# A two-layer graph network on one core: edges counted by 16 destinations in pairs of windows, other banks for the first source rows, branch arms exchanged

## The chip, the cores and the metric

One core of one Trainium2 chip. The metric is the device time of one execution in microseconds (us), median of the runs. The kernel is written for the five engines directly: each engine has a program of its own and they meet at semaphores only. TensorE is called PE in the rows (PEld is its weight load), VectorE DVE, ScalarE ACT, GpSimd POOL, SyncE SP.

## The reference

1,250 nodes with 768 features, 40,000 edges (src, dst) sorted by dst, and a self loop for each node. Two blocks, each followed by a residual and a layer norm:

```
x_norm = layer_norm(x)
out1 = gat_conv(x_norm, ...)        # 4 heads of 192; softmax over the edges of a dst
out2 = gat_conv(out1, ...)          # 2 heads of 96
x = layernorm(x + (concat([x, out2]) @ Wu + bu))
h = relu(gcn_conv(x, W1, b1))       # out[dst] += (x @ W)[src] * dinv[src] * dinv[dst]
x = layernorm(x + gcn_conv(h, W2, b2))
```

Every sum over edges depends on the graph only through how often a pair (src, dst) occurs. So the kernel first makes the dense matrix of counts, 1280 x 1280, and turns both layers into dense products with it.

## The kernel before

**Counting.** The edges lie in 313 chunks of 128; two chunks are a *unit* (157 units). The destinations are cut into 40 *windows* of W = 32, four for each of T = 10 tiles of 128. Since the edges are sorted, a window needs a short run of units. For each unit VectorE compares (`one_hots`): `src_hot`, for each edge which of 128 low source numbers it has (256 elements, two chunks), and `dst_hot`, for each edge which of 320 pairs (source tile, destination in the window) it has (640 elements). TensorE multiplies the two per chunk (`mm`, 320 columns, bf16) and adds all units of a window in one PSUM bank (`edge_window`). UW = 4 units are written out in a ring of RING = 4 slots (names `ohs_*`, `ohd_*`); what a window needs beyond them runs in a loop with run-time bounds (`xohs`, `xohd`), at least once a window. The bounds come from a small table in SBUF (`rngrow`), made at the start by VectorE from the smallest and largest destination of each chunk, and read into registers (`TENSOR_LOAD rngrow`) by TensorE and VectorE. A matmul with the identity adds the self loops. ScalarE copies the bank into `ctmp`.

**What lies between.** After each window of a tile TensorE does a quarter of the first layer's dense product (`wp`, `xT`, three matmuls, six records), after the first one also the ten transposes of the previous tile's counts (`count_transposes`); ahead of a tile it transposes the normalised rows (`normal_transposes`), and ScalarE copies them to `xT` in six pieces. The last tile does its product in two windows, twelve records each.

**Handover.** When the source scores of all tiles are there, VectorE splits them in two parts (`svec`), TensorE transposes them and broadcasts them over the partitions (`source_rows`, ten matmuls for one head into three banks), ScalarE copies the three pieces (`source_piece`), and VectorE takes 10 maxima a head (`maximum`), 40 in all, then starts the attention. Beside this TensorE does `x_transposes` and `x_wu` (the product of x with Wu).

**GCN.** A register says whether any degree is over 4096. If so, `messages` and `gcn` run in plain f32, otherwise with every number in a high and a low part. Here it is the second. In `first_layer` six column blocks f of 128 are summed over ten source tiles q: `pair(q)` does blocks 0 and 1 beside the preparation of tile q, `sums(2, q)` the third block, which uses the other banks (0, 1, 5); block 3 needs the banks of blocks 0 and 1 (2, 3, 4) back.

An engine's program is a fixed order; no scheduler is involved.

## Time and profile before

| | |
|---|---|
| three runs | 804.77, 807.14, 807.78 us; median 807.14 |
| profiled execution | 806.62 us, of it span 804.9 |
| busy in the span | PE 768.4 us, DVE 579.0, ACT 321.1, POOL 23.3 |
| counting (about 41 to 202 us) | PE full, DVE 75 to 95% |
| maxima and first attention (204 to 305) | DVE full |
| other attention, GCN (305 to 800) | PE full but for short gaps |

A busy PE is a model: its records overlap, and what a matmul costs is the distance of its start to the next start. "Idle before, releaser" at a row's end says how long the engine stood still ahead of that instruction and what ended it.

### The profile page before, as it was taken

To read this page: it belongs to the slowest core of one execution; us is meant where nothing else is said; L and a number is where in the kernel's file an instruction comes from. 1 tells how busy PE (TensorE), PEld (TensorE's weight loads), DVE (VectorE), ACT (ScalarE), POOL (GpSimd) and SP (SyncE) were. 2 spreads that over 40 slices of the span, in tenths; PEclk is the share of its full clock that TensorE was granted. 3 is DMA by queue.
4 is the path that set the end of the run, shared out by engine and by line. 5 is a ranking of instruction groups with operands and counts; after the bars stand their busy time and mean duration, and the time that the engine had idled before them with its cause. 6 is when DMAs were issued, how large, how long until landed. Compare 5 with 4: busy or idle time off the path is not lost.

```text
span 804.9 us, 11740 instructions
## 1 busy us (share of the span) xinstructions
PE 768.4 (95%) x4215; PEld 651.9 (81%) x4215; DVE 579.0 (72%) x1143; ACT 321.1 (40%) x638; POOL 23.3 (3%) x38
## 2 busy tenths in 40 slices
PE   5999999999999989999999999899999999999997
PEld 4966666665665989999966788799799999999996
DVE  2699988886899999999689999795553432403554
ACT  4537666754533334343253555562203331301000
POOL 6100000000000010000000020000000000000000
PEclk9999999999989999999989999999999999999999
DMA  9400000000000132020000510100000003000121
GB/s 314 159 2 1 1 1 2 1 1 2 1 1 0 67 133 66 1 66 1 1 0 1 184 31 1 42 1 1 1 1 1 1 0 118 1 1 1 59 79 54
DMA packets 10672, 28.15 MB, mean 35 GB/s; under 512 B 675, under 2 KB 4079, under 8 KB 10100
## 3 DMA queue, kind: packets, MB, share of 16 engines
q1 hardware_dynamic: 10612, 27.36, 9.8%
q8 instruction: 36, 0.59, 0.3%
q14 instruction: 24, 0.20, 0.1%
HBM read 23.48 MB, written 3.88 MB: 34 GB/s over the span
## 4 chain that ended last, share of the span: by engine, by line
PE 82%; DVE 11%; ACT 3%; issue 2%; DMA 1%; SPq 1%; DVEq 0%; ACTq 0%
PE ps L1231 78%; DVE att L698 4%; DVE att L737 4%; PE ps L1330 1%; PE ps L1384 1%; PE ps L1273 1%; DMA edges<-in_dst 1%; DVE out L721 1%; ACT att L1063 0%; DVE h2x L721 0%; DVE ylo_a L839 0%; ACT ctr L921 0%; ACT uB L921 0%; PE ps L1518 0%; ACT xT L946 0%
## 5 line engine op out<-in xcount | busy, mean ns | idle before, releaser
L1231 PE MATMUL ps<-g,att 128*128 128x193 f32 x800 | 133.4, 328 | 3.2 <-DVE att L698 1.5
L1231 PEld LDWEIGHTS ps<-g,att 128*128 128x128 f32 x800 | 130.3, 190 | 6.1 <-DVE att L698 3.2
L1063 ACT ACTIVATE att<-att,ssrc 128x1250 f32<-128x1250 f32 x60 | 80.1, 1338 | 97.5 <-DVE att L737 97.2
L737 DVE SCALAR_TENSOR_TENSOR att<-uB,s 128x1250 f32<-128x1250 f32 x60 | 90.7, 1515 | 0.0
L1231 PE MATMUL ps<-ctr,yhi 128*128 128x512 f32 x360 | 88.6, 353 | 1.9 <-DVE ylo_b L839 1.4
L1231 PE MATMUL ps<-wp,xT 128*128 128x388 f32 x240 | 87.5, 502 | 0.8 <-ACT xT L946 0.8
L698 DVE SCALAR_TENSOR_TENSOR att<-att,ct 128x1250 f32<-128x1250 f32 x60 | 87.3, 1456 | 1.1 <-ACT att L1063 0.9
L839 DVE TENSOR_TENSOR ylo_a<-ps,yhi 128x512 fp32r<-128x512 f32 (+2 forms) x34 | 16.1, 527 | 80.1 <-ACT yhi L921 80.1
L1231 PEld LDWEIGHTS ps<-ctr,yhi 128*128 128x128 f32 x360 | 64.1, 188 | 8.4 <-DVE ylo_b L839 1.7
L1231 PE MATMUL ps<-ctr,ylo_a 128*128 128x512 f32 (+3 forms) x288 | 70.2, 352 | 0.1
L1231 PEld LDWEIGHTS ps<-wp,xT 128*128 128x128 f32 x240 | 42.6, 190 | 24.8 <-issue 1.0
L921 ACT ACTIVATE yhi<-ps 128x384 fp32r<-128x384 f32 (+2 forms) x36 | 16.2, 530 | 98.4 <-PE ps L1231 98.4
L1231 PEld LDWEIGHTS ps<-ctr,ylo_a 128*128 128x128 f32 x288 | 51.1, 188 | 5.2 <-DVE ylo_a L832 0.4
L1231 PE MATMUL ps<-h2x,att 128*128 128x97 f32 x400 | 48.0, 277 | 4.2 <-DVE att L698 2.8
L1231 PEld LDWEIGHTS ps<-h2x,att 128*128 128x128 f32 x400 | 46.0, 192 | 6.7 <-DVE att L698 5.7
L576 DVE TENSOR_TENSOR ohs_abc<-iota,sloT 128x256 bf16<-128x256 bf16 x120 | 34.4, 287 | 21.2 <-PE ps L1231 19.9
L1231 PE MATMUL ps<-wux,xT 128*128 128x384 f32 x120 | 41.1, 499 | 0.0
L1231 PE MATMUL ps<-wux,xTd 128*128 128x384 f32 x120 | 40.7, 499 | 0.0
L1231 PE MATMUL ps<-gw2lo,yhi 128*128 128x384 f32 x120 | 40.6, 338 | 0.0
L1231 PE MATMUL ps<-gw2hi,yhi 128*128 128x384 f32 x120 | 40.4, 337 | 0.0
L1231 PE MATMUL ps<-gw1lo,yhi 128*128 128x384 f32 x120 | 40.2, 335 | 0.0
L877 DVE SCALAR_TENSOR_TENSOR hpre<-ps,dinv,gb1b 128x384 f32<-128x384 f32 x20 | 12.4, 618 | 37.8 <-PE ps L1231 37.8
(250 smaller groups left out, 1370.0 us busy)
## 6 DMA issues: line engine op xcount, KB each, us to landing
uB<-u_dram SPq DMA_DIRECT2D x4, 1280.0 KB, 6.0
wux<-in_L_gnn_Wu SPq DMA_DIRECT2D x2, 2304.0 KB, 16.2
gw<-in_L_gnn_W SPq DMA_DIRECT2D x2, 2304.0 KB, 10.3
xs<-in_x SPq DMA_DIRECT2D x1, 3456.0 KB
out<-ybuf SPq DMA_DIRECT2D x9, 384.0 KB, 2.3
w<-in_L_gnn_W SPq DMA_DIRECT2D x2, 1152.0 KB, 7.3
w2x<-in_L_gnn_W SPq DMA_DIRECT2D x1, 576.0 KB, 7.4
wuo<-in_L_gnn_Wu SPq DMA_DIRECT2D x1, 576.0 KB
```

The source lines that it names most:

```text
L576: v.tensor_tensor(src_hot, iota[:, None, :, :].to_broadcast([P, PR, P, 2]), sloT[:, bass.ds(p0, PR), None, :].to_broadcast([P, PR, P, 2]), ...
L698: v.scalar_tensor_tensor(a, a, HUGE, ct[:, q, 0:N], ALU.min, ALU.mult).then_inc(att_ready, 1)
L721: last = v.scalar_tensor_tensor(o, src, rden[:, q:q + 1], add, ALU.mult, ALU.add)
L737: v.scalar_tensor_tensor(att[:, att_place(n), 0:N], uB[:, hp % 2, 1, 0:N], s08[:, h, q:q + 1], uB[:, hp % 2, 0, 0:N], ALU.add, ALU.max).th ...
L839: last = v.tensor_tensor(rows, place(f, k)[:, a0 * P - span[0]:a1 * P - span[0]].rearrange("p (t n) -> p t n", n=P), yhi[:, a0:a1, f * P:( ...
L877: v.scalar_tensor_tensor(hpre[:, n % 2, :], ps[:, H_RING[n % 4], 0:HALF], dinv[:, q:q + 1], gb1b[:, k * HALF:(k + 1) * HALF], ALU.mult, AL ...
L921: a.activation(dst, src, ACT.Copy, **kw).then_inc(done, 1)
L1063: a.activation(at_, at_, ACT.Exp, bias=ssrc[:, h, q:q + 1]).then_inc(att_exp, 1)
L1231: return t.matmul(o, lhsT, rhs, start=start, stop=stop, **kw)
L1273: step = t.transpose(ps[:, 4 + k, c * P:(c + 1) * P], place[:, kk * P:(kk + 1) * P], identf[:, :])
L1330: last = t.transpose(ps[:, 4 + k, c * P - c0:(c + 1) * P - c0], ctmp[:, r, c, :], identf[:, :])
L1384: last = t.transpose(ps[:, xt_bank(q, k), c * P:(c + 1) * P], xs[:, q, kk * P:(kk + 1) * P], identf[:, :])
```

## The change

The windows are 16 wide (80 of them); two form a *group*, which takes the place of a window in the order of the program. A narrow window has UW = 3 fixed units, compared in one pair of VectorE instructions (768 and 960 elements) into one of four ring slots, and multiplied in six matmuls of 160 columns. Both halves of a group lie side by side in one bank, with one loop for the extra units of both, one identity matmul and one ScalarE copy. The ranges come from tables of pair numbers with fewer VectorE steps; a group has five numbers, of which TensorE reads two and VectorE four into registers. The matmul that sums the extras runs one block of weight products later. In the last group the score split (`source_scores`) and its transpose stand between the two halves; before, they stood ahead of the last window. The first source rows go to banks 7, 2, 3 in place of 4, 5, 6, the last count transposes no longer wait for them, and `x_wu(0)` runs ahead of the second source rows. TensorE's branch has the narrow arm first (VectorE's and ScalarE's are as before). In the third block five of ten passes stand ahead of the last two pairs, one between them and four behind; before, eight ahead, one between, one behind.

```
-W = 32
+W = 16
+SUB = 2
+GR = SUB * W
-UW = 4
+UW = 3
+HELD = 5
...
+        def row_bank(n):
+            return (7, 2, 3)[n] if n < 3 else 4 + n % 4
...
+            def group(q, r, w, limits):
+                gr = GPT * q + w
+                first, end, unit_a, unit_b, middle = limits
...
+                for s, unit in enumerate((unit_a, unit_b)):
+                    win = SUB * gr + s
+                    v.wait_ge(unit_used, win + 1)
+                    if win == RING - 1:
+                        v.wait_ge(wp_out, 2 * KD)
+                    one_hots(unit, UW, ring_src(win % RING), ring_dst(win % RING), vk[:, s:s + 1, :, :], kv, unit_ready)
+                    if gr + 1 < NG:
+                        nxt += group_range(v, gr + 1, *((1, 2), (3, 4))[s])
+                    elif s == 0:
+                        source_scores()
...
-                copy(ctmp[:, r, :, w * W:(w + 1) * W], ps[:, w % 2, 0:WC].rearrange("p (a b) -> p a b", b=W), win_out)
+                copy(ctmp[:, r, :, w * GR:(w + 1) * GR].rearrange("p a (s b) -> p s a b", s=SUB), ps[:, w % 2, 0:SUB * WC].rearrange("p (s a b) -> p s a b", s=SUB, b=W), win_out)
...
+            x_transposed(0)
             counts_out(T - 1)
-            x_transposed(0)
...
+                for s in range(SUB):
+                    win = SUB * gr + s
+                    src, dst = ring_src(win % RING), ring_dst(win % RING)
+                    t.wait_ge(unit_ready, win + 1)
+                    for c in range(UW * UC):
+                        last = mm(ps[:, w % 2, s * WC:(s + 1) * WC], src[:, c // 2, :, c % 2], dst[:, c // 2, :, c % 2], s == 0 and c == 0, False, skip_group_check=True)
...
+            t.wait_ge(dn_out, 2 * T + 2)
             source_rows(0, 3)
+            count_transposes(T - 1, 1)
             t.wait_ge(bc_out, 3)
-            count_transposes(T - 1, 1)
-            t.wait_ge(dn_out, 2 * T + 2)
             x_transposes(0)
+            t.wait_ge(wu_plus, KD)
+            x_wu(0)
...
-                for q in range(T - LAG):
+                for q in range(HELD):
                     sums(2, q)
-                for q in range(T - LAG, T):
-                    pair(q)
+                pair(T - 2)
+                sums(2, HELD)
+                pair(T - 1)
+                for q in range(HELD + 1, T):
                     sums(2, q)
...
-            with t.If(is_wide > 0):
+            with t.If(is_wide < 1):
+                gcn(ctr, [lambda q, c0, c1: yhi[:, q, c0:c1], ylo])
+            with t.Else():
                 gcn(ct32, [lambda q, c0, c1: y32[:, q, c0:c1]])
```

TensorE's program, the first window of a tile in the middle of the counting, before:

```order
L1231 MATMUL ps<-ohd_ab,ohs_abc 128x320 [waits unit_ready,win_out]
L1231 MATMUL ps<-ohd_ab,ohs_abc 128x320
L1231 MATMUL ps<-ohd_ab,ohs_abc 128x320 [waits unit_ready]
L1231 MATMUL ps<-ohd_ab,ohs_abc 128x320
L318 TENSOR_LOAD rngrow
L1231 MATMUL ps<-ohd_c,ohs_abc 128x320 [waits unit_ready]
L1231 MATMUL ps<-ohd_c,ohs_abc 128x320
L1231 MATMUL ps<-ohd_d,ohs_d 128x320 [waits unit_ready]
L1231 MATMUL ps<-ohd_d,ohs_d 128x320
L1315 UNCONDITIONAL_BRANCH
L1315 ISA
L1231 ISA [waits extra_ready]
```

The same place in the changed program, from the group's first matmul to the loop of the extras:

```order
L1252 MATMUL ps<-hotd_a,hots_a 128x160 [waits unit_ready,win_out]
L1252 MATMUL ps<-hotd_a,hots_a 128x160 x5
L324 TENSOR_LOAD rngrow
L1252 MATMUL ps<-hotd_a,hots_a 128x160 [waits unit_ready]
L1252 MATMUL ps<-hotd_a,hots_a 128x160 x5
L324 TENSOR_LOAD rngrow
L1340 UNCONDITIONAL_BRANCH
L1340 ISA
L1252 ISA [waits extra_ready]
L1252 ISA
L1252 REGISTER_ALU
L1252 MATMUL ps<-xohd,xohs 128x160
```

Eight wide matmuls with four waits for VectorE became twelve narrow ones with two; there are two register loads in place of one, and one step more (ISA, REGISTER_ALU) in the loop.

TensorE's program behind the last window: the source rows (`sRow_96` times `sel`), the last count transposes (`ctmp`), the first x transposes (`xs`), before:

```order
L1231 MATMUL ps<-identb 128x32
L1231 MATMUL ps<-sRow_96,sel 128x128 [waits row_out]
L1231 MATMUL ps<-sRow_96,sel 128x128 x9
L1330 MATMUL ps<-identf,ctmp 128x128 [waits win_out,bc_out]
L1330 MATMUL ps<-identf,ctmp 128x128 x9
L1384 MATMUL ps<-identf,xs 128x128 [waits dn_out]
L1384 MATMUL ps<-identf,xs 128x128 x5
L1231 MATMUL ps<-sRow_96,sel 128x128 [waits wu_plus,cp_deg]
```

And in the changed program:

```order
L1252 MATMUL ps<-identb 128x2x16
L1252 MATMUL ps<-sRow_99,sel 128x128 [waits dn_out,row_out]
L1252 MATMUL ps<-sRow_99,sel 128x128 x9
L1357 MATMUL ps<-identf,ctmp 128x128 [waits win_out]
L1357 MATMUL ps<-identf,ctmp 128x128 x9
L1407 MATMUL ps<-identf,xs 128x128 [waits bc_out]
L1407 MATMUL ps<-identf,xs 128x128 x5
L1252 MATMUL ps<-wux,xTd 128x384 [waits tp_out,wu_plus]
L1252 MATMUL ps<-wux,xTd 128x384 x5
L1252 MATMUL ps<-wux,xTd 128x384 [waits tp_out]
L1252 MATMUL ps<-wux,xTd 128x384 x5
L1252 MATMUL ps<-sRow_99,sel 128x128 [waits cp_deg]
```

The wait for the copied pieces (`bc_out`) moved from the count transposes to the x transposes, and the x product (`wux`) moved ahead of the second source rows.

## Rows read from the trace of the kernel before

**Rows 1.** The chain, counting stage: start us, us, what.

```profile
41.16 12.04 PE ps L1231 x61
...
152.41 3.49 PE ps L1231 x17
...
168.09 3.49 PE ps L1231 x17
...
184.53 1.88 ACT xT L946 x5
```

**Rows 2.** Windows: stretch, length, PE, PEld, DVE, ACT, POOL busy, clock, DMA, GB/s.

```profile
140.00:160.00 20.00, 20.00 (x112) 13.42 (x111) 15.64 (x51) 13.79 (x37) 0.00 (x0) 1.00 0.00 1
...
220.00:240.00 20.00, 18.61 (x71) 13.06 (x70) 20.00 (x29) 7.31 (x17) 0.00 (x0) 0.83 0.00 1
```

**Rows 3.** Timeline, TensorE, one counting window: start us, us, engine, what.

```profile
141.15 0.73 PE L1231 MATMUL ps<-ohd_ab,ohs_abc 128*128 128x320 bf16 x4
...
142.57 0.18 PE L1231 MATMUL ps<-identb 128*128 128x32 bf16 x1
...
142.60 2.20 PE L1231 MATMUL ps<-wp,xT 128*128 128x388 f32 x6
...
144.63 0.73 PE L1231 MATMUL ps<-ohd_ab,ohs_abc 128*128 128x320 bf16 x4
```

**Rows 4.** Timeline, VectorE, the same window's last comparisons.

```profile
143.78 0.48 DVE L577 TENSOR_TENSOR ohd_d<-vkey,key 128x640 bf16<-128x640 int16 x1
...
144.18 0.28 DVE L576 TENSOR_TENSOR xohs<-iota,sloT 128x256 bf16 x1
...
144.38 0.48 DVE L577 TENSOR_TENSOR xohd<-vkey,key 128x640 int16 x1
```

**Rows 5.** Groups of instructions: busy us, mean ns, idle before.

```profile
L1231 PEld LDWEIGHTS ps<-wp,xT 128*128 128x128 f32 x240 | 42.6, 190 | 24.8 <-issue 1.0
...
L1231 PE MATMUL ps<-xohd,xohs 128*128 x92 | 19.9, 303 | 0.6 <-DVE xohd L577 0.4 <-issue 0.2
...
L1231 PEld LDWEIGHTS ps<-ohd_ab,ohs_abc 128*128 128x128 bf16 x160 | 15.3, 97 | 12.3 <-issue 5.4 <-DVE ohd_ab L577 0.4
```

**Rows 6.** Timeline, ScalarE, copies into xT at a tile's start.

```profile
152.28 2.22 ACT L946 ACTIVATE xT<-ps,gcol 128x128 f32<-128x128 f32 x6
```

**Rows 7.** Timeline, from window 38 to the first maximum.

```profile
197.06 0.72 PE L1231 MATMUL ps<-ohd_ab,ohs_abc 128*128 128x320 bf16 x4
...
197.91 0.18 DVE L624 CAST svec<-ssrc 128x40 fp32r<-128x40 f32 x1 [2.58 <-ACT sdst L921]
...
201.66 0.46 PE L1231 MATMUL ps<-xohd,xohs 128*128 x2 [0.39 <-DVE xohd L577]
...
202.05 1.20 PEld L1231 LDWEIGHTS ps<-sRow,sel 104*128 104x128 f32 x10
...
204.15 1.46 DVE L572 CUSTOM_DVE_ANT_0 scrap<-ssB_a,mask 128x1250 bf16<-128x1250 f32 x1 [2.69 <-ACT ssB_a L921]
```

**Rows 8.** Timeline, the first x product, and where VectorE waits next.

```profile
210.25 7.91 PE L1231 MATMUL ps<-wux,xTd 128*128 128x384 f32 x24
...
261.31 0.16 DVE L736 MEMSET att<- 128x120 f32 x1 [0.20 <-PE ps L1231]
```

**Rows 9.** Timeline, the entry into the GCN part.

```profile
505.81 0.40 PE L1518 MATMUL ps<-identf,out 128*96 128x128 f32 x2 [1.61 <-DVE out L721]
...
506.79 0.42 DVE L804 TENSOR_TENSOR o2Tlo<-ps,o2Thi 96x256 fp32r<-96x256 f32 x1 [0.97 <-ACT o2Thi L921]
```

**Rows 10.** Timeline, TensorE, the last pass of the third block and behind.

```profile
566.73 0.73 PE L1231 MATMUL ps<-ctr,yhi 128*128 128x512 f32 x3
567.30 0.72 PE L1231 MATMUL ps<-ctr,ylo_b 128*128 128x512 f32 x3
568.46 0.95 PE L1231 MATMUL ps<-ctr,yhi 128*128 128x512 f32 x2 [0.44 <-DVE ylo_a L839]
...
570.82 0.44 PE L1231 MATMUL ps<-ctr,yhi 128*128 128x384 f32 x1 [1.42 <-DVE ylo_b L839]
```

More of the change, by code:

```diff
@@ L36 @@
 RING = 4
[L37 to L38 removed]
+NONE = 4096
+UW = 3
 HALF = D // 2
@@ L530, in _ @@
-            step(v.scalar_tensor_tensor(rng[:, 3:4], rng[:, 3:4], -float(UW), rng[:, 2:3], ALU.add, ALU.subtract))
+            for k, (op, pairs) in enumerate(((ALU.is_ge, pairlo), (ALU.is_le, pairhi))):
+                for s in range(SUB):
+                    last = v.scalar_tensor_tensor(cand[:, k, s, :], ps[0:NG, 6 + k, 0:EC], wlim[:, s, k:k + 1], pairs[:, :, :].rearrange("p a c -> p (a c)"), op, ALU.mult)
+            step(last)
+            v.tensor_reduce(lohi[:, 0, :], cand[:, 0, :, :], AX.X, ALU.min)
@@ L579, in window, with one_hots @@
-            def window(q, r, w, limits):
-                win = WPT * q + w
-                first, end, unit0 = limits
+            def one_hots(p0, pairs, src_hot, dst_hot, vk, kv, done):
+                v.tensor_tensor(src_hot, iota[:, None, :, :].to_broadcast([P, pairs, P, 2]), sloT[:, bass.ds(p0, pairs), None, :].to_broadcast([P, pairs, P, 2]), ALU.is_equal)
+                v.tensor_tensor(dst_hot, vk.to_broadcast([P, pairs, WC, 2]), kv[:, bass.ds(p0, pairs), None, :].to_broadcast([P, pairs, WC, 2]), ALU.is_equal).then_inc(done, 1)
@@ L583, in window @@
                 vk, kv = (vkey, vkey1, vkey2, vkey3)[w], key[:, r, :, :]
                 nxt = [end]
-                for j in range(UW):
-                    slot = (UW * w + j) % RING
-                    v.wait_ge(unit_used, UW * win + j + 1)
-                    p0 = nc.s_assert_within(v.snap((unit0 + j) * PR), 0, (UN - 1) * PR,
-                                            skip_runtime_bounds_check_because="the first unit was clamped")
-                    one_hots(p0, ring_src(slot), ring_dst(slot), vk, kv, unit_ready)
-                    if win + 1 < NW and j < 2:
-                        nxt += window_range(v, win + 1, j + 1)
+                for s, unit in enumerate((unit_a, unit_b)):
[8 more added lines that the diff above has]
+                        source_scores()
@@ L610, in tile @@
                 for w in range(3):
-                    limits = window(q, r, w, limits)
+                    limits = group(q, r, w, limits)
                     if q < T // 2 and w == 0:
@@ L1008, in tile @@
                     transposed(q, xT[:, r, :, :])
-                for w in range(WPT):
+                for w in range(GPT):
                     if q < T // 2 and w == 1:
                         deviations(2 * q + 1, min(2 * q + 3, T))
-                    if w == WPT - 1 and not last:
+                    if w == GPT - 1 and not last:
                         a.wait_ge(rstd_ready, q // 2 + 2)
@@ L1350, in tile @@
                     t.wait_ge(cst_out, 1)
-                for w in range(WPT):
-                    limits = edge_window(q, w, limits)
-                    if w == 2 and last:
-                        t.wait_ge(vec_ready, 1)
-                        t.wait_ge(cp_deg, 3 * q + 4)
-                        t.transpose(ps[0:VR, 5, 0:P], svec[:, :].bitcast(F32), identf[:, :]).then_inc(row_ps, 1)
+                for w in range(GPT):
+                    limits = edge_group(q, w, limits)
                     if not last or w < 2:
```

182 lines of the change are left out of this document (90 added, 92 removed).

## The prediction

> **What bounds the kernel now.** I read the windows table first, to see which engine is full in which stage, then the chain, then the timeline inside one tile. The profiled execution took 806.62 us (0.5 us under the median of 807.14), 804.9 of it span, so 1.7 us lie around the span. The change touches four places: the counting stage, from 41 us on [rows 1], the handover from it to the maxima at 197 to 261 us, the entry into the GCN part at 505 us, and its third block at 567 us.
>
> In the counting stage TensorE is full: 20.00 of 20 us, at the full clock of 2.4 GHz, while VectorE has 15.64 and ScalarE 13.79 [rows 2]. Two tiles in a row are 15.68 us apart in the chain, and nothing but TensorE stands in them; only the last tile has a ScalarE piece [rows 1]. One window shows how the time is laid out: its first counting matmul starts at 141.15, the identity matmul at 142.57, the dense product at 142.60, the next window at 144.63 [rows 3]. So ten counting matmuls of 320 columns (four fixed units and one extra, two chunks each) take 1.42 us, 0.142 us each; the identity matmul takes 0.03, the dense product (six records) 2.03; together 3.48. 0.142 is 0.133 for 320 columns at 2.4 GHz and 0.009 over. Their records are longer (0.73 for four) because they overlap; starts count.
>
> **The change, part by part.** *Counting matmuls.* Before, 46 extra rounds ran (92 records) [rows 5] beside 160 fixed units: 412 matmuls by 0.142 = 58.5 us. After, each group of two 16-wide windows has two times six matmuls of 160 columns. Counting the seed-0 destinations, 9 of the 80 narrow windows touch a fourth unit, never two in one group, so the loop's minimum of one extra round holds for every group: 14 matmuls by 40 groups = 560. Their price is the main unknown, since no bf16 matmul of 160 columns runs now. From below: half of 0.142 = 0.071. From above: a load of f32 weights in front of each, as for the row broadcasts, where ten loads take 1.20 us, some 0.112 each [rows 7]. I take 0.076 (0.067 for 160 columns and the 0.009 over). It is nearer the lower end because a bf16 load record lasts 97 ns and an f32 one 190 [rows 5]: if an f32 load occupies its path for 0.112, the bf16 one that is 0.093 shorter occupies it for about 0.02, well under 0.067.
>
> A page bears on it and speaks against me. The Trainium skill, "TensorE: Matmul & The Clock Gate", section "Back-to-back issue gap", gives about 81 ns per load and matmul at 128 columns in a real stream; worked out from it, an estimate of 0.094 for 160 columns, and a count stage saving about 9 us less than mine. It also gives 131 ns at 512 columns, which this trace refutes: 320 columns already take 142 ns.
>
> Up to window 38 (38 by 5 units and 6 second extras) are 196 units = 392 matmuls = 55.7 us before, 38 by 14 by 0.076 = 40.4 after: 15.3 saved. Against it: ScalarE's six copies into xT start at 152.28 and take 2.22 [rows 6]; the third, for which the dense product waits, is done near 153.4 plus a handover. The window before it starts near 152.3 and would end at 153.4 rather than 153.7, so TensorE waits about 0.15 in each of 8 tiles: 1.2. In the last tile it already waits for all six copies (the piece at 184.53) [rows 1]; the 0.35 won there is lost. Net 13.75.
>
> *VectorE's one-hots.* A 640-element comparison takes 0.40 start to start, a 256-element one 0.20 [rows 4]: 0.067 and 0.52 ns an element. So 768 elements take 0.467, 960 take 0.567, 320 take 0.233. A group costs 2 by 1.034 and 0.433 = 2.50 us, against 3.0 for a five-unit window. TensorE's group is 14 by 0.076, 0.03 and 2.03 = 3.12. VectorE stays behind the cover, also with the moments (at most some 2.6 us a tile): 12.9 against a tile of about 14.2. The slots now hold two groups, so it can run ahead.
>
> *Range tables, start.* The new table steps end, like the old, well before the first counting matmul at 41.16 [rows 1], which waits behind weight products. Costed at nothing; without that cover a late table would cost its lateness once, under 1 us.
>
> *Last group and source rows.* Before, the score split waits for the dense result and is finished 1.3 us after window 38 starts (197.06; the split starts at 197.91), and only then does VectorE begin the whole last window; TensorE waits for it up to the extra matmuls at 201.66 and starts the source rows at 202.05, 5.0 after 197.06 [rows 7]. After, the first half of the last group is built ahead of the split: 1.3, then 1.03 for the second half, 0.43 for the extra, 0.3 of handover and 0.2 on TensorE: 3.2. Gain 1.8. The maxima follow 2.1 later in both. The new banks free the count transposes from waiting for three copies; that is TensorE's slack only. VectorE is full from 204.15 to 261.3, where it waits 0.20 for TensorE [rows 8]; that 0.2 goes. So the stage start moves, its length not.
>
> *Branch arms.* TensorE idles 1.61 us between the last attention matmul and 505.81; behind it VectorE waits 0.97 for the chain through ScalarE [rows 9]. The transposes need only the first collected pair, done by then, so I read the idle as the jump over the first arm. VectorE and ScalarE keep their order of arms, and VectorE has its collects to finish, so at most 0.97 can be won, at least 0; I take 0.5. By the Trainium skill, "Runtime: NRT & Kernel Launch", section "Instruction fetch mechanics", a taken branch out of the fetched window costs a fetch; the idle agrees.
>
> *Third block.* Now one pass of it (two parts, 0.57 us each from start to start) follows the last pair, then TensorE idles 0.44 and 1.42 until the low halves are written [rows 10]: 1.86. The last pair ends near 566.9, the banks are free at 570.8: 3.9 to cover. After, four passes stand there, 4 by 1.15 = 4.6 us. The stall goes: 1.85.
>
> Sum: 13.75 + 1.8 + 0.2 + 0.5 + 1.85 = 18.1 us. 806.62 - 18.1 = 788.5; beside the median, 807.1 - 18.1 = 789.0.
>
> **Rivals.** (1) *The narrow matmul costs more than its columns, 0.09 us.* Half way between 0.071 and 0.112; each 0.01 costs 5.3 us ahead of window 38. At 0.09: 7.4 less, 796.5. The short load record speaks against it. The Trainium skill's figure above would be this case. (2) *The load holds it at 0.112.* 532 by 0.036 = 19.2 lost, less the 1.55 of waits that vanish: 806.6. Same speed as now. (3) *The reordered product delays the maxima.* The first x product (24 records, 7.91 us) [rows 8] now runs ahead of the second source rows, which VectorE needs some 14 us after it starts (ten maxima at 1.46 or less) [rows 7]. At the full clock they are ready at about 12. But the granted clock there is 0.83 in the mean [rows 2]; were all of this product at 1.2 GHz, it takes 15.8 and VectorE waits some 5 us: 794. (4) *Slower: TensorE's instruction stream becomes the bound.* Its register loads double (one a window, two a group), the loop has an address more to work out, and only 1.06 us of matmuls cover them. At the last window the extra matmuls already start 0.3 us behind their data [rows 7]. It decides from 0.45 us a group (18.1 over 40); at 0.65 it is 26 - 18 = 8 slower, 815. Against it: in a middle window ten matmuls follow each other with no gap through the same loop [rows 3]. (5) VectorE loses its two elements per cycle in the three-unit forms: 2 by 0.9 us a group more, VectorE binds at 4.3 us a group, some 25 us slower than now; no reason for it in the inner pairs of elements, which stay.
>
> **How the numbers follow.** Forecast (784 to 792 of its own) 0.56; (1) 0.13; (3) 0.12; (2) 0.08; (4) and (5) together 0.06; something unnamed 0.05, mostly on the faster side. Its own range is the branch (0 to 0.97), 0.071 for the matmul (2.7 better) and waits of ScalarE up to 0.3 a tile. 0.5% is 4 us, about what a measurement of this kernel can tell from no change. Faster by over 0.5%: forecast, (1), (3) and the unnamed, 0.86. Within it: (2), 0.08. Slower: 0.06. The range runs from 783 to 798, which takes in (1) and (3) and leaves out (2), (4) and (5).
>
> **What would show it.** Right: narrow counting matmuls 0.076 apart, tiles 14.2 us apart at the full clock, VectorE waiting for slots and never waited for; source rows 3.2 us after the last but one group starts; VectorE full for 57 us behind; a transposing TensorE at once behind the last attention matmul; no idle at the third block's end. Wrong: starts 0.09 or more apart; an issue gap before each extra round; a VectorE wait for source rows 14 us into the maxima; a low granted clock in the counting stage.

## The result

| kernel | median of the runs | profiled span | ratio to the kernel before |
|---|---|---|---|
| before | 807.78 us (5 runs) | 804.9 | |
| changed | 799.06 us (5 runs, 798.55 to 799.13) | 797.4 | 0.9894 [0.9873, 0.9915] |
| forecast | 789.0 (783 to 798) | | |

The change is 1.1% faster, 8.7 us, and the forecast was 18.1. (Seventeen later runs of the kernel before have a median of 806.2, by which the gain is 7.1.) Of the forecast sum, 10.6 us are missing (18.1 less the 7.5 by which the span shrank in the profiles). To find them I cut both traces at the same four events: the first counting matmul, the first maximum, the end of the last attention matmul, and the first `o2Tlo` of VectorE. Each number below is the time between two such rows. Spans are printed to 0.1 us, so the last column is good to 0.05.

| | first counting matmul | to first maximum | to last attention matmul | to o2Tlo | to the end |
|---|---|---|---|---|---|
| before | 41.16 | 162.99 | 300.05 | 2.59 | 298.11 |
| changed | 45.20 | 151.98 | 300.28 | 4.03 | 295.91 |
| difference | +4.04 | -11.01 | +0.23 | +1.44 | -2.20 |
| forecast | 0 | -15.55 | -0.2 | -0.5 | -1.85 |

**The start.** These are rows of the timeline of the changed kernel: GpSimd, VectorE and TensorE up to the first counting matmul.

```profile
4.04 1.87 POOL L484 IOTA pairlo<- 40x320 f32 x1
5.97 1.85 POOL L485 IOTA pairhi<- 40x320 f32 x1
...
12.64 5.83 POOL L498 IOTA vkey<- 128x320 int16 x6
12.61 0.55 DVE L521 TENSOR_SCALAR shi<-edges 128x384 int32<-128x384 int32 x1 [12.61 <-POOL wcol L493]
...
15.05 0.73 DVE L527 CAST slor<-slo 128x384 f32<-128x384 int32 x1
15.71 2.91 DVE L530 TENSOR_SCALAR diag<-identf,dminmax 128x128 f32<-128x128 f32 x6
18.76 0.45 PE L1281 MATMUL ps<-identf,shir 128*128 128x128 f32 x1 [3.31 <-DVE diag L530]
...
22.92 8.94 PE L1252 MATMUL ps<-w2x,w1T 96*128 96x194 f32 x48
...
45.20 1.02 PE L1252 MATMUL ps<-hotd_a,hots_a 128*128 128x160 bf16 x12 [0.47 <-issue]
```

Two pair tables of 1.87 and 1.85 us stand where one table of 0.46 stood, so VectorE, which had started with the edges at 12.02, now starts with its constants at 12.61. GpSimd's window tables, now six, run from 12.64 to 18.47, right beside VectorE's `diag`, which takes 2.91 us (1.26 before). Seen closer, two of the six `diag` instructions end just behind each table, here at 17.66 behind a table that ends at 17.51:

```profile
16.52 0.99 POOL L498 IOTA vkey<- 128x320 int16 x1
16.63 1.03 DVE L530 TENSOR_SCALAR diag<-identf,dminmax 128x128 f32<-128x128 f32 x2
```

TensorE waits 3.31 for `diag`, and the weight products then start at 22.92. The 4.04 us add up so: the transposes start 2.62 late (0.59 of the constants, 0.38 of the CAST, 1.65 of `diag`), 1.06 go in TensorE's work from there to the `xh` transposes, and 0.36 in what stands ahead of the first counting matmul, where TensorE is idle for 0.47 without a wait that the profile shows.

**The counting.** TensorE in the second group of the changed kernel:

```profile
49.31 0.59 PE L1252 MATMUL ps<-hotd_b,hots_b 128*128 128x160 bf16 x6
49.74 0.59 PE L1252 MATMUL ps<-hotd_c,hots_c 128*128 128x160 bf16 x6
50.17 0.30 PE L1252 MATMUL ps<-xohd,xohs 128*128 x2
50.31 0.18 PE L1252 MATMUL ps<-identb 128*128 128x32 bf16 x1
50.34 2.20 PE L1252 MATMUL ps<-wp,xT 128*128 128x388 f32 x6
52.37 0.31 PE L1252 MATMUL ps<-hotd_a,hots_a 128*128 128x160 bf16 x2
```

Its windows table for five tiles from 60.51 on (length, busy time and records of PE, PEld, DVE, ACT and POOL, granted clock, DMA):

```profile
60.51:75.39 14.88, 14.59 (x101) 10.54 (x101) 12.74 (x32) 10.44 (x29) 0.00 (x0) 1.00 0.01 2
75.39:90.56 15.17, 14.98 (x100) 10.57 (x101) 13.17 (x33) 10.45 (x29) 0.00 (x0) 1.00 0.01 2
90.56:106.05 15.49, 15.06 (x100) 10.57 (x101) 13.31 (x35) 10.45 (x29) 0.00 (x0) 1.00 0.01 2
106.05:120.78 14.73, 14.54 (x101) 10.50 (x101) 12.16 (x30) 10.45 (x29) 0.00 (x0) 1.00 0.01 2
120.78:135.11 14.33, 14.16 (x101) 10.47 (x101) 12.15 (x29) 10.27 (x28) 0.00 (x0) 1.00 0.00 1
```

And VectorE in its tile 3, one group and the step behind it:

```profile
93.96 0.56 DVE L593 TENSOR_TENSOR hots_a<-iota,sloT 128x768 bf16<-128x768 bf16 x1
94.43 0.65 DVE L594 TENSOR_TENSOR hotd_a<-vkey,key 128x960 bf16<-128x960 int16 x1
95.00 0.55 DVE L593 TENSOR_TENSOR hots_a<-iota,sloT 128x768 bf16<-128x768 bf16 x1
95.47 0.65 DVE L594 TENSOR_TENSOR hotd_a<-vkey,key 128x960 bf16<-128x960 int16 x1
96.59 0.29 DVE L593 TENSOR_TENSOR xohs<-iota,sloT 128x256 bf16 x1 [0.47 <-issue]
96.85 0.32 DVE L594 TENSOR_TENSOR xohd<-vkey,key  x1
97.09 0.16 DVE L570 RECIPROCAL rstd<-sd 128x2 f32<-128x2 f32 x1
```

Six narrow matmuls take 49.74 - 49.31 = 0.43 us, 0.072 each: against the ten of before [rows 3] this is the lower end of my bounds. A group is 3.06 long (3.12 forecast) and the later tiles 14.33. But the four tiles before 120.78 are 14.73 to 15.49. In the later ones TensorE waits for ScalarE's copies into xT: behind the first identity matmul of a tile (134.76) the dense product starts at 135.11, 0.35 later and not 0.03. And a group costs VectorE 3.13 us (97.09 - 93.96), not the 2.50 I worked out, since 0.47 of idle time stands ahead of `xohs`, as it does not in the window of [rows 4].

**The handover.** TensorE and VectorE from the last but one group on:

```profile
189.24 1.02 PE L1252 MATMUL ps<-hotd_a,hots_a 128*128 128x160 bf16 x12
...
190.09 0.18 DVE L600 CAST svec<-ssrc 128x40 fp32r<-128x40 f32 x1 [4.01 <-ACT sdst L942]
...
191.61 0.60 PE L1252 MATMUL ps<-hotd_c,hots_c 128*128 128x160 bf16 x6 [0.64 <-DVE hotd_c L594]
...
192.65 0.40 PE L1252 MATMUL ps<-xohd,xohs 128*128 x2 [0.43 <-issue]
...
194.17 0.41 PE L1252 MATMUL ps<-xohd,xohs 128*128 x2 [1.12 <-DVE xohd L594]
194.58 0.18 PE L1252 MATMUL ps<-identb 128*128 128x32 bf16 x1
194.72 1.09 PE L1252 MATMUL ps<-sRow,sel 104*128 104x128 f32 x6
```

The rows start 5.5 us after the last but one group, not 3.2 (before 5.0, [rows 7]). There are two extra rounds in the last group, where I had counted one. The first maximum (197.18) is then 7.94 behind that group, before 204.15 - 197.06 = 7.09.

**The entry to the GCN part.** TensorE's transposes, ScalarE, VectorE's last collect, its `o2Tlo`, and TensorE behind it:

```profile
497.29 0.38 PE L1543 MATMUL ps<-identf,out 128*96 128x128 f32 x2
...
497.77 0.38 ACT L942 ACTIVATE o2Thi<-ps 96x256 fp32r<-96x256 f32 x1 [5.07 <-PE ps L1543]
...
498.53 0.54 DVE L742 SCALAR_TENSOR_TENSOR out<-ps,rden,b2b 128x96 f32<-128x96 f32 x2
...
501.49 0.42 DVE L825 TENSOR_TENSOR o2Tlo<-ps,o2Thi 96x256 fp32r<-96x256 f32 x1 [2.42 <-issue]
...
501.96 0.44 PE L1252 MATMUL ps<-wuohi,o2Thi 96*128 96x384 f32 x1 [4.29 <-DVE o2Tlo L825]
```

TensorE is there at once, as forecast, but VectorE, whose branch nobody had touched, stands still for 2.42 us without a wait that the profile shows, and TensorE waits 4.29 (1.05 before, [rows 9]).

### The profile page after: what moved, and what is told of

Its sections match the earlier page's. It is cut to its first block, busy times and chain, and to the rows that moved or that the text cites. A ratio compares the mean times of both kernels' runs of the same rounds, so it can differ in the third digit from the quotient of the medians.

```text
span 797.4 us, 11900 instructions
## 1 busy us (share of the span) xinstructions
PE 755.4 (95%) x4365; PEld 658.0 (83%) x4365; DVE 562.2 (71%) x973; ACT 321.9 (40%) x638; POOL 28.6 (4%) x43
## 4 chain that ended last, share of the span: by engine, by line
PE 73%; DVE 13%; issue 8%; ACT 4%; POOL 1%; DVEq 0%; POOLq 0%; ACTq 0%
PE ps L1252 71%; DVE att L758 4%; DVE att L719 4%; PE ps L1357 1%; ACT xT L967 1%; DVE out L742 1%; DVE scrap1b L589 1%; ACT g L1022 1%; PE ps L1407 1%; ACT att L1084 0%; DVE h2x L742 0%; DVE mx L589 0%; DVE diag L530 0%; DVE scrap L589 0%; ACT ctr L942 0%
## 5 line engine op out<-in xcount | busy, mean ns | idle before, releaser
L1252 PE MATMUL ps<-h2x,att 128*128 128x97 f32 x400 | 49.7, 287 | 2.6 <-DVE out L742 1.4
L1252 PEld LDWEIGHTS ps<-h2x,att 128*128 128x128 f32 x400 | 48.8, 203 | 4.0 <-DVE att L719 3.2
L1252 PEld LDWEIGHTS ps<-wux,xT 128*128 128x128 f32 x120 | 23.6, 201 | 15.4 <-issue 2.1
```

The source lines that it names most:

```text
L1252: return t.matmul(o, lhsT, rhs, start=start, stop=stop, **kw)
```

## The experiments

Each is compared with the changed kernel by the same cuts; the run times stand beside, and each ratio is to the kernel before. Profiles differ even where no edit reaches: over the kernels with the changed kernel's start, the first counting matmul is at 43.8 to 45.4, and the third column is 299.0 to 300.3. What follows rests on the stage that an edit touches.

### The start

`e2_gate`, GpSimd's window tables behind `diag`:

```
             pool.wait_ge(const_a, 1)
+            pool.wait_ge(diag_ready, 1)
             for w, table in enumerate((vkey1, vkey2, vkey3)):
```

> The changed kernel with GpSimd's six window tables (vkey1 to vkey3, 12.64 to 18.47) started only when VectorE's diag is done. Theory: the six diag instructions take 2.91 us instead of 1.26, and the CAST ahead of them 0.73 instead of 0.35, because GpSimd writes its tables at the same time; then diag takes 1.3, TensorE's transposes start at about 16.8 (before 16.14, changed kernel 18.76), and the counting starts 1.7 to 2.0 us earlier, at about 43.3. What then delays is VectorE's later steps that now meet the tables (15 to 21 us). Rival: diag is slow for another reason (clock, layout), it stays at 2.9 and the counting starts at 45.2.

Measured: 795.37 us, ratio 0.9858 [0.9833, 0.9884], 3.7 us under the changed kernel. Its timeline, VectorE and TensorE:

```profile
15.03 0.35 DVE L528 CAST slor<-slo 128x384 f32<-128x384 int32 x1
15.30 1.26 DVE L531 TENSOR_SCALAR diag<-identf,dminmax 128x128 f32<-128x128 f32 x6
...
16.70 0.30 PE L1282 MATMUL ps<-identf,shir 128*128 128x128 f32 x1 [0.57 <-DVE diag L531]
...
40.48 0.73 PE L1253 MATMUL ps<-hotd_a,hots_a 128*128 128x160 bf16 x8 [0.46 <-issue]
```

`diag` is back at 1.26, the CAST at 0.35, and the counting starts 4.7 us earlier, more than twice what I expected. The transposes start 2.06 earlier; the rest is the clock: in the changed kernel TensorE stood still for 3.31 us ahead of 18.76, and its granted clock is 0.50 from 18 to 23 us and 0.85 from 23 to 28. Here it waits 0.57 and keeps the full clock: the two `diag` products take 1.49 us against 2.78. But they took 2.78 in the kernel before too, at a granted clock of 0.67 from 16 to 18 us and 0.79 from 18 to 23. So 1.3 of the 4.7 us is time that the kernel before loses as well, and no part of the forecast's miss; and `b3_pad97` below, with the start of the kernel before, has them in 1.49 and the first counting matmul at 39.96.

`e3_k2`, the sum of the extras back ahead of weight block 2:

```
-                if k == 3:
+                if k == 2:
                     t.wait_ge(keys_out, 1)
```

> The changed kernel with the matmul that sums the extras (base_ps) back ahead of weight block 2 instead of 3, nothing else. The numbers it needs are ready at 28.2, and block 2 starts at 28.3 to 28.4. Theory: VectorE's moments stand behind base_ps, so the square root, xh and the first normal transposes and the range row are 3.3 us late because of this placement; base_ps runs at 28.4, the TENSOR_LOADs of the ranges follow 3 us earlier, TensorE's waits for xh (1.17) and ahead of the first counting matmul (0.47) go: counting starts at 43.6 to 44.0, 1.2 to 1.6 us gained. Rival: the start is late by diag alone (3.1 of the 4.0 us), xh comes from a table load that waits elsewhere: less than 0.4 gained.

Measured: 798.84 us, ratio 0.9888 [0.9867, 0.9909]; first counting matmul at 44.55. The expectation fell. The range numbers are written 3.3 us earlier (29.21 against 32.53), but TensorE still waits 1.16 for `xh`: ScalarE's square root stands behind a certain copy of the weight products, and that copy does not move. The rival holds; the gain is at most 0.6. (`c2_more` below also moves that square root, and TensorE's wait for `xh` is gone.)

### The counting

`e1_loads` and `e10_loads2` put VectorE's register loads elsewhere in a group; the second:

```
-                    if gr + 1 < NG:
-                        nxt += group_range(v, gr + 1, *((1, 2), (3, 4))[s])
+                    more = gr + 1 < NG and s == 0
+                    one_hots(..., lambda: nxt.extend(group_range(v, gr + 1, 1, 2) if more else []))
+                    if more:
+                        nxt += group_range(v, gr + 1, 3, 4)
```

> The changed kernel with VectorE's four register loads of a group put elsewhere: one between the two comparisons of the first half, two behind the first half, one between the comparisons of the second half, none directly ahead of the loop of the extras. Theory: the idle time ahead of xohs (16.6 us over 34 times, some 0.45 each) is the two loads that now stand last ahead of the loop; in tiles 1 to 4, where VectorE also has the moments, it makes VectorE late for TensorE (tile periods 14.88, 15.17, 15.49, 14.73 against 14.33). Then the idle time ahead of xohs falls below 6 us, tiles 1 to 4 come down to 14.4 or less, and the kernel gains about 1.9 us. Rival: the idle time is the loop's own start (its address arithmetic), the loads are hidden: xohs idle stays at 14 us or more and the periods do not move; or the periods of tiles 1 to 4 come from ScalarE, and stay though the idle time goes.

> The changed kernel with all four register loads of VectorE within the first half of a group (two between its comparisons, two behind), none behind the second half. With one of them between the comparisons of the second half, the idle time ahead of xohs was still 0.27, a new one of 0.18 stood ahead of the second half, and the group took VectorE 3.18 us as before. Theory: the loop's start (branch, addresses) takes about 0.8 us from the last load on and is hidden only if the last load is more than that ahead; here it is 1.03 ahead: the idle time ahead of xohs goes below 0.1, a group takes VectorE 2.9 to 3.0, tiles 1 to 4 come down by 0.3 to 0.6 each, 1.5 us in all. Rival: the loop's start needs the engine drained, its idle time stays at 0.25 or more wherever the loads are, and the periods do not move.

Measured: 799.35 us (0.9898 [0.9877, 0.9919]) and 798.32 us (0.9903 [0.9887, 0.992]). With `e1_loads` the idle time ahead of `xohs` goes from 15.7 to 10.0 us, with `e10_loads2` to 1.2, but new idle time of 6.3 us stands ahead of the comparisons and a group still takes VectorE 3.13 (92.55 to 95.68). The periods of tiles 1 to 4 stay (14.81, 15.30, 15.43, 14.68 in the second). Both theories on the place of the loads fell: wherever the loads stood, the group cost VectorE the same. No run leaves the loads or the loop out, so which of them holds VectorE up stays open.

`e9_spread` leaves them and takes the other part of VectorE's work out of the early tiles:

```
-                    if q < T // 2 and w == 0:
-                        moments(*pair(q))
+                    if q % 2 == 0 and w == 0:
+                        moments(*pair(q // 2), q + 2 if q else 1)
+                    if q % 2 == 1 and w == 0 and q + 2 < T:
+                        sums_of(q + 2, q + 3, q + 2 == T - 1)
...
-                    if q < T // 2 and w == 1:
-                        deviations(2 * q + 1, min(2 * q + 3, T))
+                    if q % 2 == 0 and w == 1:
+                        deviations(q + 1, min(q + 3, T))
```

> The changed kernel with the layer-norm moments of the ten tiles spread: one tile's sums in each counting tile (two in tile 0), instead of two in each of the tiles 0 to 4; nothing left out. Moving the register loads did not change the periods of tiles 1 to 4 (14.8, 15.3, 15.6, 14.7 against 14.33), it only moved VectorE's idle time within a group. Theory: a group costs VectorE 3.13 us, not 2.50, whatever the place of the loads, so that with 2.6 us of moments VectorE needs about 15.4 us in tiles 1 to 4 and is the bound there. Spread, it needs 14.1 or less: tiles 1 to 8 all take 14.3 to 14.5, and the kernel gains 2.5 to 2.9 us. Rival: the periods come from ScalarE (its square roots and table loads) or from the extra matmuls' issue: the long tiles then are tiles 2, 4, 6, 8, or stay 1 to 4, and the sum of the periods falls by less than 1 us.

Measured: 795.92 us, ratio 0.987 [0.9846, 0.9895]. The periods are 14.33 in the odd tiles and 14.63, 14.70, 14.64, 14.71 in the even ones, where the square root and the second part of the moments now stand; tiles 1 to 8 take 1.6 us less and the way to the first maximum is 2.04 shorter (2.5 to 2.9 were expected). So VectorE was the bound in tiles 1 to 4. The rest of about 0.3 in the even tiles is left; whether ScalarE's table loads or VectorE's moments hold it was not tried.

### The handover

`e7_middle` ends the last group's loop at the first half's limit. It leaves out the extra round for destinations 1264 to 1279, which no node has:

```
-                with t.Fori(first, end) as n:
+                with t.Fori(first, end if gr + 1 < NG else middle) as n:
```

(and the same on VectorE.)

> The changed kernel where the last group's loop of the extras ends at the first half's limit, so that its second round, for the window of destinations 1264 to 1279 that no node has, is not run. Theory: that round costs what the chain shows, 194.17 - 192.65 = 1.52 us, once; the source rows follow the first round at once and start at about 193.2 instead of 194.7, and the maxima 1.5 us earlier; kernel 1.5 us faster. Rival: the round is hidden behind something that the rows wait for anyway (the score transpose, ScalarE's row copy): rows start less than 0.4 us earlier.

Measured: 796.74 us, ratio 0.9877 [0.9854, 0.9901]; to the first maximum 150.17 instead of 151.98. VectorE's extra pair and TensorE behind it:

```profile
190.56 0.33 DVE L594 TENSOR_TENSOR xohd<-vkey,key  x1
...
191.44 0.40 PE L1252 MATMUL ps<-xohd,xohs 128*128 x2 [0.43 <-issue]
...
191.99 1.69 PE L1252 MATMUL ps<-sRow,sel 104*128 104x128 f32 x10
```

The rows still start 3.96 us behind the last but one group (188.03), not 3.2. The second half takes what I had put down for it, 1.07 from 189.22 to 190.29; but the rows start 1.14 behind VectorE's last instruction for the group (190.85), where I had 0.5.

`e12_lastg` puts the score split behind the whole group as well:

```
-                    elif s == 0:
-                        source_scores()
...
+                if gr + 1 == NG:
+                    source_scores()
```

> The changed kernel without the second extra round of the last group, as in the run before that left it out, and with VectorE's score split behind the whole last group instead of between its halves. VectorE idles 4.01 us ahead of the split, waiting for ScalarE's last scores, while the second half and the extra of the last group stand behind it. Theory: that order is what is left of the handover's loss: with the split last, TensorE waits for neither hotd_c (0.64) nor the extra, the source rows start 1.9 to 2.6 us behind svec's second part instead of 4.2 (3.0 with the round left out), and the first maximum is 2.7 to 3.2 us earlier than in the changed kernel counted from the first counting matmul (151.98). Rival: the rows then wait for the transposed scores through ScalarE: gain over leaving out the round (1.81) below 0.4.

Measured: 795.86 us, ratio 0.9867 [0.9834, 0.9901]; to the first maximum 148.60, 3.38 less than in the changed kernel and 1.57 less than with the round alone left out. VectorE and TensorE there:

```profile
187.03 0.32 DVE L594 TENSOR_TENSOR xohd<-vkey,key  x1
...
189.89 0.19 DVE L600 CAST svec<-ssrc 128x40 fp32r<-128x40 f32 x1 [2.54 <-ACT sdst L942]
...
191.64 1.08 PE L1252 MATMUL ps<-sRow,sel 104*128 104x128 f32 x8
```

VectorE is through with the last one-hots 2.5 us before it has the scores. In the changed kernel they queue behind a wait of 4.01. The rows now start 2.6 us behind the last but one group (189.04), where I had forecast 3.2 for the changed kernel.

### The branches

`e4_arms` (VectorE's and ScalarE's arms exchanged too; VectorE's edit is shown) and `e5_pearm_old` (TensorE's back as before):

```
-            with v.If(is_wide > 0):
-                messages(wide_y)
-            with v.Else():
-                taken = messages(narrow_y)
+            with v.If(is_wide < 1):
+                messages(narrow_y)
+            with v.Else():
+                taken = messages(wide_y)
```

> The changed kernel with the arms of VectorE's and ScalarE's branches exchanged too (narrow one first). Theory: the 2.42 us that VectorE idles ahead of o2Tlo is its jump over the wide arm. Then o2Tlo follows the last collect (499.07) by less than 0.5, TensorE's 4.29 us of waiting falls to about 2, its clock does not fall, and everything behind is 2.0 to 3.5 us earlier: some 796.5. Rival: VectorE's idle time is not the jump but something else between the collects and the branch (reading the register, the DMAs that SyncE issues at 499.10): it stays above 2, and nothing is gained.

> The changed kernel with TensorE's branch as before (wide arm first), nothing else. Theory: TensorE's 1.6 us idle ahead of the transposes returns, but VectorE's own jump ends later (2.42 us behind its last collect), so that the end moves by less than 0.4 us: TensorE's exchange alone is worth nothing here. Rival A: it is worth 0.5 us or more. Rival B: VectorE's idle time was 0.97 at most before the change because both engines' jumps are related (they fetch at the same time or not): with TensorE's arms back, VectorE's falls to 1 us and this kernel is about 2 us faster than the changed one.

Measured: `e4_arms` 794.68 us, ratio 0.9842 [0.9821, 0.9864]; `o2Tlo` 1.53 behind the last attention matmul, no idle time ahead of it. Of its 4.4 us the entry is 2.5; 1.2 lie in the third column, which the edit does not reach. `e5_pearm_old` 798.74 us, ratio 0.9902 [0.9878, 0.9925]: TensorE's transposes start 2.49 behind, `o2Tlo` 4.05 behind, as with the new order. So VectorE's jump is the loss, and TensorE's exchange alone gives nothing beside it. With the arms exchanged the jump is not gone: it stands at the end of the narrow arm, over the wide one. There, in `e4_arms`, VectorE is idle for 2.10, where the changed kernel has 0.83 of waiting for TensorE:

```profile
728.07 0.62 DVE L931 SCALAR_TENSOR_TENSOR ybuf<-ps,dinv,xs 128x384 f32<-128x384 f32 x1 [2.10 <-issue]
```

TensorE waits for nothing in that part, so the end does not move by it.

But the kernel before has the same arms, and loses less. `b1_pearm` is that kernel with TensorE's arms exchanged, `b2_rest` with all three and the third block's new order:

> The kernel before with TensorE's arms exchanged alone. In the kernel before, VectorE's o2Tlo starts 2.59 us behind the last attention matmul; in every kernel with the changed counting it is 4.03 to 4.33, with TensorE's arms either way. Theory: VectorE's jump over its wide arm costs what it costs, and in the kernel before it ended within 0.97 us by its place in the program (a shorter or longer way to the arm): here o2Tlo stays 2.6 or falls to 2.1 at best (the 0.5 of my prediction), and the kernel is the same as before within 0.6 us. Rival: the two jumps meet: with TensorE's arm first, VectorE's idle time grows to 2.4 here too, o2Tlo at 4.0, and the kernel is 1.4 us slower than before, so that the exchange itself made the loss.

> The kernel before (wide windows, its start, its handover) with all three branches narrow arm first and the third block in the new order. Theory: the entry gains 1.1 us (o2Tlo 1.5 behind the last attention matmul instead of 2.6) and the block 1.9 to 2.6: 3.0 to 3.7 us faster than before, 803.5 to 804.2; the counting and the start stay as before. Rival: the block's new order gives nothing by itself (less than 1 us), and its 2.2 us in the changed kernel come from elsewhere in that stage.

Measured: `b1_pearm` 806.46 us, ratio 0.9997 [0.9983, 1.0012], `o2Tlo` 1.75 behind, VectorE still for about 0.15. So the exchange gives 0.84 at its place there, more than the 0.5 of my expectation at best, and the end does not show it: the stage behind is 1.1 longer, with a granted clock of 0.91 from 560 to 580 us (1.00 before). `b2_rest` 802.42 us, ratio 0.9949 [0.9932, 0.9966]: 1.52 behind, and 295.11 to the end: the block and the clock behind the entry are worth 3.0. The rival of `b2_rest` fell.

`e11_pad160` and `b3_pad97` (97 in place of 160) change only where the branch stands in VectorE's program:

```
+            for _k in range(160):
+                v.sem_inc(filler, 1)
             v.wait_ge(const_a, 1)
```

> The changed kernel with 160 more instructions in VectorE's program, all at its very start (each only raises a counter that nobody reads), where VectorE waits for the edges anyway. VectorE's branch to the GCN part is then its instruction 1655, as it is instruction 1654 in the kernel before; in the changed kernel it is 1495. Theory: what VectorE's jump over its wide arm (229 instructions) costs depends on the branch's place in the engine's program: about 0.15 at 1654, 2.42 to 2.72 at 1495. Here the idle time ahead of o2Tlo falls to under 0.5, o2Tlo starts 1.5 to 1.8 behind the last attention matmul, and the kernel is 2 to 4 us faster than the changed one, like the one with VectorE's arms exchanged (794.7). Rival: the cost comes from something else in the changed kernel (what the DMA queues carry, the other engines' programs): it stays at 2.4 or more.

> The kernel before with 97 more instructions in VectorE's program, at its start as in the run beside it. Its branch is then instruction 1751, which is 1495 and 256. The Trainium skill, Runtime: NRT & Kernel Launch, section Instruction fetch mechanics, says that instructions are fetched in blocks of 256; by that the branch stands in its block where the changed kernel's stands. Theory by the place in a block: VectorE's idle time behind its last collect grows to 2.4 or more, o2Tlo starts 3.9 to 4.3 behind the last attention matmul instead of 2.59, and the kernel is 1.3 to 1.7 us slower than before. Rival: the place in a block is not what counts: o2Tlo stays at 2.6, and the time is that of before within 0.6 us.

Measured: `e11_pad160` 797.44 us, ratio 0.9882 [0.9851, 0.9914]; `b3_pad97` 809.8 us, ratio 1.004 [1.0023, 1.0057]. VectorE's last collect and `o2Tlo` in the timeline of `e11_pad160`:

```profile
499.85 0.54 DVE L745 SCALAR_TENSOR_TENSOR out<-ps,rden,b2b 128x96 f32<-128x96 f32 x2
500.55 0.42 DVE L828 TENSOR_TENSOR o2Tlo<-ps,o2Thi 96x256 fp32r<-96x256 f32 x1
```

The same two in that of `b3_pad97`:

```profile
503.77 0.54 DVE L724 SCALAR_TENSOR_TENSOR out<-ps,rden,b2b 128x96 f32<-128x96 f32 x2
506.74 0.42 DVE L807 TENSOR_TENSOR o2Tlo<-ps,o2Thi 96x256 fp32r<-96x256 f32 x1 [2.43 <-issue]
```

The same jump over 229 instructions costs 0.15 us from instruction 1655 and 2.4 from 1495, and in the old program 2.4 from 1751 (places are counted in the built programs). (The first gains less in all than `e4_arms`, since its 160 instructions run to 16.20 and hold up the start by 1.0; the entry itself gains 2.26. The second is 3.6 slower. In its profile 1.45 is the entry; the stage behind is 2.45 longer, with a granted clock of 0.83 from 500 to 520 us and 0.91 from 560 to 580, for 0.91 and 1.00 before; its start happens to be 1.2 shorter.) Both expectations on the place held, and the rivals fell.

### The third block

`e6_held_old` puts its passes back as before.

> The changed kernel with the third block's order as before (eight passes ahead of the last two pairs, one between, one behind). Theory: the stall of 1.86 us at the block's end returns, and nothing else moves: 1.8 to 1.9 us slower than the changed kernel, about 801. Rival: the new order gave more than the stall, since the trace shows 2.7 us between the start of that stage and the end: 2.5 us or more slower; or less, since VectorE or ScalarE then wait elsewhere.

Measured: 802.55 us, ratio 0.9944 [0.9917, 0.997], 3.5 us above the changed kernel. From `o2Tlo` to the end 298.52, against 295.91 to 296.45 with the new order: 2.1 to 2.6. That is the stall and 0.2 to 0.8 more, which stays open. Its TensorE rows show the stall of [rows 10] again, to the hundredth:

```profile
563.53 0.94 PE L1252 MATMUL ps<-ctr,yhi 128*128 128x512 f32 x2 [0.44 <-DVE ylo_a L860]
...
565.89 0.44 PE L1252 MATMUL ps<-ctr,yhi 128*128 128x384 f32 x1 [1.42 <-DVE ylo_b L860]
```

### The causes together

`c1_all` is the changed kernel with the pair tables behind `const_a`, the gate of `e2_gate`, and the edits of `e9_spread`, `e4_arms` and `e7_middle`. `c2_more` adds the edits of `e12_lastg` and `e3_k2`, and ScalarE's first square root and `xh` two copies earlier:

```
-                    if n == 7:
+                    if n == 5:
                         deviations(0, 1)
-                    if n == 8:
+                    if n == 6:
```

> The changed kernel with the repairs that the runs so far point to, together: GpSimd writes the pair tables behind the constants that VectorE waits for, and the six window tables when diag is done; the moments spread over the tiles; all three branches with the narrow arm first; the last group's second extra round left out. Theory: the four act at different places and add up: start -4.5 to -5, tiles 1 to 4 about -2, last group -1.8, entry to the GCN part -2.5: 11 us below the changed kernel, 788 (786 to 790), ratio to the kernel before about 0.977. Rival: part of it is given back where another engine is next (ScalarE's copies in the counting tiles, a lower clock at the handover): 791 or more.

> The combined kernel (GpSimd's tables, spread moments, narrow arms first, no second extra round) with three more: the score split behind the last group, base_ps ahead of weight block 2, and ScalarE's first square root and xh two copies earlier, so that TensorE's 1.29 us wait for xh goes. Theory: start 1.2 to 1.3 earlier (first counting matmul at 38.7), handover 1.0 to 1.2 earlier: 787.0 to 787.6 from the 789.65 of the combined kernel. Rival: the combined kernel's own times go from 787.2 to 794.3 with granted clocks of 0.974 to 0.987, so that a gain of 2.4 us disappears in where the half clock falls: the trace shows both gains and the time does not.

Measured: 789.65 us (0.9801 [0.9769, 0.9832]; its runs lie between 787.15 and 794.29) and 786.19 us (0.9734 [0.9706, 0.9761]), 2.7% under the kernel before. By the cuts, `c2_more` has 38.57, 147.24, 302.99, 1.53, 295.47. `c1_all` is inside its 786 to 790 but not at 788, and what it lacks is in the third number (302.97 for 300.28; `c2_more` has it too): from the transpose of the second layer's scores to its first attention matmul it takes 40.42 us (391.39 to 431.81) for 37.67 (400.04 to 437.71), and the granted clock in two windows of 20 us there is 0.83 and 0.83 for 0.91 and 0.91. The rival of `c1_all` is thus partly right: 2.7 us of the repairs are given back, at a lower granted clock, in a part that no edit touches. Why the clock falls there is not shown.

## Why the prediction was wrong

**Counting matmuls: right.** 0.072 us, inside 0.071 to 0.076, so rivals (1) and (2) did not occur. The Trainium skill, "TensorE: Matmul & The Clock Gate", section "Back-to-back issue gap", gives about 81 ns at 128 columns; this trace has less for 160, and the estimate of 0.094 made from it fell with it. ScalarE's copies were sized too low: 0.33 a tile (14.33 less four groups of 3.06, against 15.68 less four windows of 3.48), not 0.15.

**VectorE's one-hots: the step that failed in this stage**, "VectorE stays behind the cover, also with the moments: 12.9 against a tile of about 14.2". The comparisons cost what I worked out (0.47 and 0.57), but not the group: 3.13 for 2.50, since 0.55 more goes by ahead of the extra pair, where a loop's start and, in the changed kernel, two register loads stand, and the extra pair takes 0.50 for 0.43. Four groups, 2.6 of moments and the key are 15.4 us. I had weighed the instruction stream for TensorE alone (rival 4), not for VectorE. The stage up to the last but one group gained 11.86 for 13.75. Tiles 1 to 4 are together 2.9 us longer than four of 14.33; without that it would have gained 14.8, since the cheaper matmul outweighs the copies. Spreading the moments gives 2.04 back.

**Range tables, start: the largest failure**, 4.0 of the 10.6 us, for a term put at nothing. "Costed at nothing; without that cover a late table would cost its lateness once, under 1 us" looked at the table steps and their cover in TensorE, and not at what else GpSimd does meanwhile. The constants are late by 0.59; the rest is VectorE held up beside GpSimd (1.65 in `diag`, 0.38 in the CAST), about 1.1 of TensorE at half clock behind the longer wait, and 0.36 ahead of the first counting matmul. `e2_gate` takes away the second and the third (and 1.3 that the kernel before lost too); the last stays (0.46 idle there).

**Last group and source rows:** forecast +1.8, measured -0.85. Of the 2.65 missing, 1.8 is a wrong count: the empty window 1264 to 1279 gets a round of its own (`e7_middle`). The rest is TensorE behind the extra pair, 1.14 where I had 0.5, and 0.1 in the pair itself. (The waits also cost clock: it is 0.54 in the changed kernel from 195.0 to 197.2 us, 1.00 before at that step.) The second half behind the split, 1.03, was sized rightly; that it need not stand there at all (1.57 by `e12_lastg`) is a gain that the forecast did not have.

**Branch arms:** "at most 0.97 can be won, at least 0". The floor was wrong. For TensorE the reading was right (`b1_pearm`: 0.84), but I took VectorE's jump as a constant of its arms; it depends on the branch's place in the program, which a shorter counting moved by 159 instructions. The loss is 1.44 in the entry.

**Third block: right in mechanism**, 2.1 to 2.6 for 1.85, of which the surplus stays open. **Rival (3)** did not occur: the second source rows are there at 209.9, VectorE needs them at about 211, and it never waits. The range failed all the same: 799.06 lies above 798, by none of the rivals. That it comes so near to (1), 796.5, is luck.

## What to carry to other kernels

When an edit lengthens or moves the work of an engine that nobody waits for (GpSimd's tables, here 5.83 us of them), look at what runs beside it in that window and not only at who waits for its result. Take a group's time on each engine from the distance of its starts, not from the sum of its comparisons, since register loads and a loop stand between them, and add what only some tiles carry, before calling an engine covered. A long jump in a program is to be priced with its place, and not from a trace of another program. Putting the common arm first moves the jump to that arm's end; it helps where, as here, nobody waits for the engine at that place.

## What the runs showed of the hardware

- VectorE's `tensor_scalar` of 128x128 f32 takes 0.21 us alone and 0.49 in the mean beside GpSimd's IOTAs, a CAST of 128x384 0.35 and 0.73; beside the same IOTAs the reductions, the integer `tensor_scalar` (0.55) and the two-input `shir` (0.56) are not slowed. The 0.49 is no slower pace: each table holds one `diag` up to its end, and the next slips in behind it (0.15 past the table's end for the two). GpSimd loses nothing, 5.83 us for six tables against 5.80 in `e2_gate`. The Trainium skill, SBUF — State Buffer, section Who interferes with whom, says that some VectorE modes and GpSimd exclude each other for a whole instruction; the trace agrees.
- A taken branch over 229 VectorE instructions costs 0.15 us or 2.4 to 2.7 by its place alone, and the place 256 instructions on costs the same 2.4. The Trainium skill, Runtime: NRT & Kernel Launch, section Instruction fetch mechanics, has blocks of 256 instructions and a stall when the target is outside the two that are held. The period agrees; a jump of 229 can leave its block only for the next one, so a stall within the two blocks is what the rule does not give. The jumps at the narrow arm's end add two places, 1724 (2.10, `e4_arms`) and 1883 (1.99, `b2_rest`). Modulo 256 the cheap places are 118 and 119, the dear ones 91, 188 and 215. All of them would fit if a jump cost this whenever its target lies in another block than the branch; no run tried to tell.
- A matmul of 160 bf16 columns with its own weights costs 0.072 us, six of them 0.43.
